# A mixing kernel from four fp32 matmuls over a masked attention, instead of 32 bf16 matmuls over parts that nine transfers spread

## What is computed

```python
h = gelu(embedding @ W0 + b0); h = gelu(h @ W1 + b1)
att = softmax((h @ W2 + b2) / T)                       # (64, 8)
agg_w = einsum('bk,koi->boi', att, weight[..., 0])     # (64, 64, 64)
agg_b = att @ bias_k
mixed = einsum('boi,bih->boh', agg_w, x) + agg_b[:, :, None]
# x + fp8(mixed) @ fp8(weight).T, with one scale for all of `mixed`
# and one for all of the 1024 x 1024 weight (largest absolute value / 448)
```

## Time and profile before

| | |
|---|---|
| runs | 527.64 us median, 527.1 to 528.81 |
| profiled execution | 530.63 us, of which 528.8 us is the span from the first to the last instruction |
| TensorE (PE) | busy 96% of the span, 3480 matmuls |
| VectorE (DVE) | busy 78% |
| ScalarE (ACT) | busy 46% |
| GpSimd (POOL) | busy 11% |
| largest shares of the chain that ended last | PE L1181 40%, PE L1155 19%, PE L1171 15%, DVE L804 5% |

### The profile page before, as it was taken

The page is one execution under the profiler, slowest core; times in us unless marked ns, Lnnn a source line. Parts: engine busy times, 40 slices in busy tenths (PEclk is TensorE's granted clock), DMA queues, the critical chain, the costliest instruction groups (busy, mean ns, idle before and its releaser), DMA issues.

```text
span 528.8 us, 9489 instructions
## 1 busy us (share of the span) xinstructions
PE 510.2 (96%) x3480; PEld 284.7 (54%) x3512; DVE 414.1 (78%) x524; ACT 244.2 (46%) x286; POOL 59.3 (11%) x68
## 2 busy tenths in 40 slices
PE   5799999899999999999999999999999999999997
PEld 4444454355555555555555555555555555555563
DVE  7799999877877777777777777777777777777652
ACT  3469898655344444444444444444444444442310
POOL 5266776011000000000000000000000000000000
PEclk9999999999999999999999999999999999999999
DMA  7999591146666666665656565656656666566532
GB/s 220 382 390 403 206 337 55 58 103 134 189 199 187 183 185 184 182 180 180 180 180 180 180 180 180 180 180 180 180 180 180 183 182 180 181 189 190 193 121 79
DMA packets 85651, 100.61 MB, mean 190 GB/s; under 512 B 34468, under 2 KB 67046, under 8 KB 85638
## 3 DMA queue, kind: packets, MB, share of 16 engines
q1 hardware_dynamic: 84610, 99.41, 59.9%
q0 software_dynamic: 656, 0.82, 0.9%
q10 hardware_dynamic: 372, 0.20, 0.1%
HBM read 58.41 MB, written 32.75 MB: 172 GB/s over the span
## 4 chain that ended last, share of the span: by engine, by line
PE 77%; DVE 12%; DMA 4%; issue 3%; SPq 2%; ACT 1%; POOL 1%; ACTq 0%; DVEq 0%; POOLq 0%
PE pair L1181 40%; PE pair L1155 19%; PE pair L1171 15%; DVE stat L804 5%; DMA Y<-in_L_ffn_weight_dram 2%; DMA work<-work 2%; PE pair L1055 1%; DVE work L729 1%; DVE work L819 1%; DVE work L921 1%; DVE Y L819 1%; DVE work L732 1%; PE pair L1145 1%; SPq L336 1%; POOL fixed L489 1%
## 5 line engine op out<-in xcount | busy, mean ns | idle before, releaser
L1181 PE MATMUL pair<-f1T,work 128*128 128x512 f16 x1024 | 231.0, 379 | 0.0
L1181 PEld LDWEIGHTS pair<-f1T,work 128*128 128x128 f16 x1024 | 98.9, 98 | 113.5 <-DVE work L928 0.2
L608 ACT ACTIVATE work<-Y,consts 128x1024 bf16 (+1 forms) x29 | 33.3, 1148 | 185.7 <-DVE work L902 185.7
L921 DVE TENSOR_TENSOR work<-Y,work 128x512 f16<-128x512 f16 (+1 forms) x64 | 71.2, 1119 | 48.0 <-ACT work L641 46.9
L1155 PE MATMUL pair<-f0T,work 128*128 128x512 bf16 x435 | 98.6, 379 | 1.8 <-DMA work<-work 0.3
L1171 PEld LDWEIGHTS pair<-taps,work 128*128 128x128 f16 x1536 | 88.3, 98 | 8.7 <-issue 0.9
L1171 PE MATMUL pair<-taps,work 128*128 128x128 f16 x1536 | 91.2, 219 | 0.6 <-issue 0.5
L934 DVE TENSOR_TENSOR Y<-pair,Y 128x512 f32 (+1 forms) x64 | 43.9, 686 | 44.4 <-PE pair L1181 44.4
L641 ACT CAST work<-Y 128x512 f16 (+1 forms) x64 | 69.6, 1137 | 19.3 <-DVE Y L911 15.6
L1155 PEld LDWEIGHTS pair<-f0T,work 128*128 128x128 bf16 x464 | 45.3, 98 | 55.1 <-DMA work<-work 0.6
L1055 PE MATMUL pair<-Y,work 128*128 128x512 f32 x128 | 61.2, 613 | 0.4 <-ACT Y L581 0.4
(11 more groups left out here) (157 smaller groups left out, 242.4 us busy)
## 6 DMA issues: line engine op xcount, KB each, us to landing
Y<-in_x_dram SPq DMA_DIRECT2D x64, 512.0 KB, 3.9
out_dram<-Y SPq DMA_DIRECT2D x31, 512.0 KB, 3.8
split_rows<-work SPq DMA_DIRECT2D x30, 520.0 KB, 2.6
work<-split_rows SPq DMA_DIRECT2D x30, 520.0 KB, 3.9
Y<-in_L_ffn_weight_dram SPq DMA_DIRECT2D x8, 512.0 KB, 9.0
Y<-in_L_ffn_W_q_dram SPq DMA_DIRECT2D x5, 512.0 KB, 15.1
work<-in_L_ffn_W_q_dram SPq DMA_DIRECT2D x3, 512.0 KB, 15.2
work<-work SPq DMA_DIRECT2D x8, 65.0 KB, 3.9
```

The lines of the kernel that those rows point to most:

```text
L921: nc.vector.tensor_tensor(split[:, r, s, 1], v[:, r, :], split[:, r, s, 0], ALU.subtract)\
L1181: last = mm(ps[2 + h][:, :], y1s[n][:, e, k, :], f1T[:, k, h * H:(h + 1) * H], start=False, stop=(e == 1 and k == KT - 1), skip_group_chec ...
```

## The change

The expert weights stay as loaded, in 64 partitions, one for a pair of expert `k` and group `c`. The attention is written eight times over (`attR`, 64 columns `(k c)`), turned once, and multiplied by a mask `own_c` (1 where the row's group is `c`) into `attM`, 64 rows by `(c, sample)` = 512 columns. One fp32 matmul for each 128 columns of `wkf`, four in all, then contracts over the 64 rows; a row contributes to its own group's columns alone. The split into bf16 parts, the nine transfers and the fillers behind the softmax fall away.

```diff
-            return pair[m][par * C:(par + 1) * C, :].rearrange("p (j t b) -> p b t j", t=T, b=NB)[:, b]
+            return pair[m][par * C:(par + 1) * C, :].rearrange("p (q c t b) -> p b t q c", q=2, c=KC, t=T)[:, b]
...
-        turns0 = {3 * r + 6: r for r in range(R8)}
+        turns0 = {3 * r + 7: r for r in range(R8)}
... SP
             for r in range(3):
                 load_w0(r)
-            for e in range(2):
-                sp.wait_ge(wk_parts, (1, 3)[e])
-                for i in range(3):
-                    sp.dma_start(wkp9[3 * i + e:KP:9, :], wkp[:, e, :]).then_inc(ld["wkp"], 16)
             load_w0(3)
+            load_mixing(0)
+            sp.wait_ge(mbk_zero, 1)
+            for b in range(NB):
+                sp.dma_start(mbk2[0:KR:KC, b * C:(b + 1) * C], cbk).then_inc(ld["mbk"], 16)
             load_w0(4)
-            for b in range(NB):
-                sp.dma_start(mbk2[:, b * C:(b + 1) * C], cbk).then_inc(ld["mbk"], 16)
             load_w0(5)
-            load_mixing(0)
+            load_mixing(1)
             load_w0(6)
             load_w0(7)
...
-                if n == 3:
+                if n == 5:
                     sp.wait_ge(mix_mm, 2)
+                    sp.wait_ge(mlp_mm, 6)
... POOL (its two loads of convw move ahead of the identity)
+            nc.gpsimd.memset(mbk2, 0.0).then_inc(mbk_zero, 1)
...
-            pool.wait_ge(wk_parts, 4)
-            for i in range(3):
-                pool.dma_start(wkp9[3 * i + 2:KP:9, :], wkp[:, 2, :]).then_inc(ld["wkl"], 16)
... ACT (its load of wkf moves behind the four small ones)
-            for m, par in ((0, 0), (0, 1), (1, 0)):
+            for m in range(2):
                 act.wait_ge(mix_mm, m + 1)
                 for b in range(NB):
-                    ev = nc.scalar.copy(mix_dst(m, par, b), mix_src(m, par, b))
+                    ev = nc.scalar.copy(mix_dst(m, 0, b), mix_src(m, 0, b))
...
-                if t == 2:
+                if t == 5:
                     act.wait_ge(w_step, 2)
-                if t % 3 == 2 and t <= 20:
-                    scale_w0(t // 3 + 1)
+                if t % 3 == 2 and 5 <= t <= 23:
+                    scale_w0(t // 3)
... DVE
+            nc.vector.tensor_reduce(own_c, ident[0:KR, 0:KR].rearrange("p (k c) -> p c k", k=K), AX.X, ALU.add)\
+                .then_inc(own_made, 1)
...
-            nc.vector.tensor_scalar(att, ex, rinv, None, ALU.mult).then_inc(mlp_ev, 1)
+            nc.vector.tensor_scalar(attR.rearrange("p (k c) -> p k c", k=K),
+                                    ex.unsqueeze(2).to_broadcast([B, K, KC]), rinv, None, ALU.mult).then_inc(mlp_ev, 1)
+            dve.wait_ge(mlp_mm, 5)
+            dve.wait_ge(own_made, 1)
+            nc.vector.tensor_tensor(attM, ps[6][0:KR, 256:256 + B].unsqueeze(1).to_broadcast([KR, KC, B]),
+                                    own_c.unsqueeze(2).to_broadcast([KR, KC, B]), ALU.mult).then_inc(mlp_ev, 1)
...
-            for r in range(1, 5):
-                largest_w0(r)
-            place_last()
-            for r in range(5, R8):
+            largest_w0(1)
+            largest_w0(2)
+            for m in range(2):
+                place_odd(m)
+            for r in range(3, R8):
                 largest_w0(r)
... PE
             for q in range(4):
-                for j in range(8):
-                    o2 = 8 * q + j
-                    last = mm(ps[q][:, j * B:(j + 1) * B], wkp9[:, o2 * 2 * C:(o2 + 1) * 2 * C],
-                              attpT, start=True, stop=True)
+                last = mm(ps[q][:, :], wkf[:, q * 2 * C:(q + 1) * 2 * C], attM.rearrange("p c b -> p (c b)"),
+                          start=True, stop=True)
...
-                    if t == 1 and h == 0:
-                        pe.wait_ge(w_red, R8 + 2)
-                        mm(ps[7][:, 128:129], ones, w_all, start=True, stop=True).then_inc(w_pe, 1)
+                    if t == 3 and h == 0:
+                        pe.wait_ge(w_red, R8 + 1)
+                        nc.tensor.transpose(ps[7][0:1, 0:P], w_part, ident[:, :]).then_inc(w_pe, 1)
...
-            keep_clock(10)
-            pe.wait_ge(placed_act, 3)
-            pe.wait_ge(placed_dve, 1)
+            pe.wait_ge(placed_act, 2)
+            pe.wait_ge(placed_dve, 2)
             for t in range(T):
                 mixed_tile(t)
-                if t == 0:
-                    pe.wait_ge(w_red, R8 + 1)
-                    nc.tensor.transpose(ps[7][0:1, 0:P], w_part, ident[:, :]).then_inc(w_pe, 1)
-                if t == 1:
+                if t == 3:
+                    pe.wait_ge(w_red, R8 + 2)
+                    mm(ps[7][:, 128:129], ones, w_all, start=True, stop=True).then_inc(w_pe, 1)
```

More of the change, by code:

```diff
@@ L81, in mix_src @@
         def mix_src(m, par, b):
-            return pair[m][par * C:(par + 1) * C, :].rearrange("p (j t b) -> p b t j", t=T, b=NB)[:, b]
+            return pair[m][par * C:(par + 1) * C, :].rearrange("p (q c t b) -> p b t q c", q=2, c=KC, t=T)[:, b]
         def mix_dst(m, par, b):
-            o = b * C + 32 * m + par
-            return mixw[b * C:(b + 1) * C, :, o:o + 31:2]
+            rows = mixw[b * C:(b + 1) * C, :, b * C:(b + 1) * C]
+            return rows.rearrange("p t (c m q o) -> p m o t q c", c=KC, m=2, q=2)[:, m, par]
         def held(eng, value):
@@ L106, in adaln_ffn_kernel @@
         mixw = work[:, 0:T * P].rearrange("p (t m) -> p t m", t=T)
-        KP = 9 * K
-        wkp9 = Y[0:KP, 20 * L:22 * L].bitcast(bf16)
         KC = C // K
         KF = C * C // KC
[L113 to L118, removed]
+        KR = K * KC
+        wkf = work[0:KR, 5 * L:5 * L + KF]
+        attM = work[0:KR, 6 * L:6 * L + KC * B].rearrange("p (c b) -> p c b", c=KC)
         wide_taps = f0T[:, 0, 0:CG * R8 * 4].bitcast(fp32).rearrange("p (c j) -> p c j", c=CG)
@@ L130, in adaln_ffn_kernel @@
         mw2 = mlp[:, 832:840]
-        att = mlp[0:B, 840:848]
-        attT = mlp[0:K, 848:912]
+        attR = mlp[0:B, 848:848 + KR]
+        own_c = mlp[0:KR, 912:912 + KC]
         rowb = mlp[0:1, 976:984]
@@ L137, in adaln_ffn_kernel @@
         convraw = work[:, 9088:9088 + CG * TAPS].rearrange("p (c k) -> p c k", c=CG)
-        mbk2 = f0T[0:K, R8 - 1, 0:2 * P].bitcast(fp32)
+        mbk2 = f0T[0:KR, R8 - 1, 0:2 * P].bitcast(fp32)
         zs = small[:, 7 * P:8 * P]
@@ L202, in taps_part @@
             return taps16[:, e, :, :, 4 * q:4 * q + 4].rearrange("p h g r a -> p (h g) r a")
-        ld = {n: sem("ld_" + n) for n in ("emb", "mw0", "mw1", "mw2", "ctw", "mbk", "wk", "wkp", "wkl", "fcol", "zs", "b0", "b1",
+        ld = {n: sem("ld_" + n) for n in ("emb", "mw0", "mw1", "mw2", "ctw", "mbk", "wk", "fcol", "zs", "b0", "b1",
                                           "convw", "window")}
@@ L220, in adaln_ffn_kernel @@
         mlp_ev = sem("mlp_ev")
-        wk_parts = sem("wk_parts")
+        own_made = sem("own_made")
+        mbk_zero = sem("mbk_zero")
         taps_made = sem("taps_made")
@@ L348, in _ @@
                 for t in range(2 * n + 1, 2 * n + 3):
-                    load_mixing(t)
-                if n == 3:
+                    if t > 1:
+                        load_mixing(t)
+                if n == 5:
                     sp.wait_ge(mix_mm, 2)
+                    sp.wait_ge(mlp_mm, 6)
                 load_w1(n)
@@ L445, in _ @@
         def _(pool):
+            for b in range(NB):
+                pool.dma_start(convraw[b * C:(b + 1) * C], convw).then_inc(ld["convw"], 16)
             nc.gpsimd.memset(ident[:, :], 0.0).then_inc(ident_zero, 1)
@@ L536, in _ @@
         def _(act):
-            act.dma_start(wkf, cwk.rearrange("k (c o) i a -> (k c) (o i a)", c=KC)).then_inc(ld["wk"], 16)
             row = lambda a: a.rearrange("(a n) -> a n", a=1)
@@ L741, in clear_mixw @@
                 nc.vector.memset(mixw[:, n * R8:(n + 1) * R8, :], 0.0).then_inc(mixw_zero, 1)
[L743 to L752, removed]
+            clear_mixw(0)
+            clear_mixw(1)
+            dve.wait_ge(ident_made, 1)
+            nc.vector.tensor_reduce(own_c, ident[0:KR, 0:KR].rearrange("p (k c) -> p c k", k=K), AX.X, ALU.add)\
+                .then_inc(own_made, 1)
+            clear_mixw(2)
+            clear_mixw(3)
             def largest_w0(r):
@@ L785, in scales, with place_odd @@
                 dve.wait_ge(step, 2)
-            def place_last():
+            def place_odd(m):
                 dve.wait_ge(mixw_zero, 4)
-                dve.wait_ge(mix_mm, 2)
+                dve.wait_ge(mix_mm, m + 1)
                 for b in range(NB):
-                    ev = nc.vector.tensor_copy(mix_dst(1, 1, b), mix_src(1, 1, b))
+                    ev = nc.vector.tensor_copy(mix_dst(m, 1, b), mix_src(m, 1, b))
                 ev.then_inc(placed_dve, 1)
@@ L1024, in _, with turned_tap_rows @@
             keep_clock(16)
-            pe.wait_ge(att_parts, 4)
-            nc.tensor.transpose(ps[1][:, :].bitcast(bf16)[0:KP, 0:B], attp9,
```

(22 more changed lines are left out.)

24 lines of the change are left out of this document (3 added, 21 removed).

## The result

The change takes **532.22 us** (median of 5 runs, 531.91 to 534.23) against 527.64: ratio 1.0094 [1.0069, 1.0119]. It is slower by 4.6 us, outside the range that was given. The profiled execution took 533.73, its span is 531.3.

What follows compares the result with a forecast made beforehand. The prediction took a weight transfer to bound the first stage until 24.1 us, then DVE from the weight's scale on. Gains of 0.8 (earlier scale) and 0.56 (end wait) made 1.4 off 527.64: 526.2 us, range 524.6 to 529.3.

Steps and rivals of the forecast that it cites:

- The nine transfers: First-stage queue: dropping them brings later transfers 5.6 us forward; last weight piece lands at 19.8, tile 3 at 23.9.
- The rival that the nine cost only their bytes: First-stage queue: only 1.5 us saved, tile 3 lands at 28.0, S 30.4, time 530.4; chance 0.08.
- I take 16, because they run without a pause: End of the four mixing matmuls on PE: 16 us, between 14.2 at the full clock and 17.6 at half.
- the forecast's own slow case: Mixing matmuls at the half clock to their end, tiles at full: PE is last and S = 26.9.
- S: Moment DVE makes the weight's scale in the first stage: 27.1 before, forecast 26.3, a gain of 0.8 us.
- The placing copies: Behind the mixing matmuls: two on ACT at 0.63 each, two on DVE at 0.70, ready at 17.7.
- The fourth rival: The change gives nothing: placing copies' four-part strides make the second pair take 2.8, not 1.4; 527.3 in the middle; chance 0.10.
- What comes last: Before S: tile 3 of x, landing at 23.9, is last, after DVE's maxima (23.6) and PE's tiles 0 to 2 (22.9).
- The first rival: PE's half clock holds into the tile mixing until 24.2: S = 29.3, time 529.3, slower by 1.6; chance 0.15.
- The third rival: Queue gains more: tile 3 lands by 22.5, matmuls at full clock, DVE's maxima bind; S = 24.9, time 524.9; chance 0.17.
- The sum against the median: Whole kernel: 1.4 us gain taken from the median 527.64, 3.0 below the profiled execution's 530.63, giving 526.2.
- Behind S and the tail: After S: other edits cost nothing; DVE's 0.56 us wait for PE before the last three maxima goes, lower bound 0.

Runs made afterwards that it cites:

- c0_before: The kernel before, unchanged, run and profiled again: 528.47 us over 12 runs, profiled execution 527.69.
- e3_rows128: The change with its four mixing matmuls over 128 rows instead of 64, the added rows being zeros: 529.73 us, ratio 1.0021 to the kernel before.
- e12: e10 without the fillers ahead of tiles 20 and 21: 527.11 us, ratio 0.9959 to the kernel before.
- e2_endfill: The change with eight filler matmuls of 512 columns where PE idles at the first stage's end: 532.11 us, ratio 1.0075 to the kernel before.
- e1: The change with PE turning the last weight piece before tile 28 again, not behind it: 533.97 us, ratio 1.0099 to the kernel before.
- e4: The change with the placing copies' two inner loops exchanged, writing neighbours 8 bytes apart within a pair: 532.55 us, one execution.
- e6: The change with the turn and spreading of the weight's maxima a tile earlier, behind half of tile 2: 533.31 us, ratio 1.0093 to the kernel before.
- e9: The change with e4's copy loops and e2_endfill's fillers, matmuls still over 64 rows: 532.42 us, ratio 1.0065 to the kernel before.
- e5: The change with the placing copies' tile loop innermost, writing in steps of 512 bytes: 531.28 us, one execution.
- e7: The change with 128-row matmuls, e4's loops, ten fillers before the first tile, the fourth weight maximum before placing, and e2_endfill's fillers: 528.87 us, ratio 1.0002.
- e10: e7 with the maxima's turn and ACT's zeros copy a tile earlier, and fillers ahead of tiles 20 and 21: 526.27 us, ratio 0.9947 to the kernel before.
- e11: e7 with 10 and 20 fillers ahead of tiles 20 and 21: 529.49 us, ratio 1.0014 to the kernel before.

## Why the prediction was wrong

- **The nine transfers: right.** The last piece and tile 3 landed at 19.4 and 23.2. The rival that the nine cost only their bytes, with tile 3 at 28.0, is refuted. In c0_before the same reckoning gives 3.6 instead of 5.6 for the nine, and tile 3 lands at 27.3, so their size varies between executions; 27.3 less 1.5 is still far from 23.2.
- **"I take 16, because they run without a pause": the step that failed.** The matmuls ended at 17.65, the worse of the two ends. What stood ahead of the rise in the kernel before were turns, fillers and most of a tile over 128 rows; four matmuls over 64 rows are no substitute, and e3_rows128 shows that in one edit. The same step let the tiles run at the full level. They were at the lower one until 23.0, and the 14 passes took 7.72 us, not 6.1. Even the forecast's own slow case, the matmuls at the lower level to their end and the tiles at the full one, gave S = 26.9. That is 2.2 too early: 1.6 for these passes, 0.8 for their start, at 20.02 and not 19.3, less 0.2 for the turn and the spreading.
- **The placing copies: a term mis-sized.** Costed at 0.63 and 0.70 as before, they take 1.08 and 1.09. That is most of the 0.8 of the tiles' start. The new step of the writes stood in the diff. The fourth rival had this at up to twice the price, with little weight.
- **What comes last.** Tile 3's transfer should have been last. It was PE, by its own work: 17.65, 19.84, 20.02 + 7.72, S 29.06. The first rival had this mechanism, and its working gave 29.3; it was given 0.15. That its S came so near is in part luck: it had the copies too short (placing ready at 19.2, measured 19.84) and the rise too late (24.2, measured 23.0). Its time, 529.3, was too low by the next point.
- **The third rival's sum.** The maxima of DVE at 21.8 would give S = 23.3 with the 1.5 for turn and spreading. The 24.9 that stands there is tile 3 landing at 22.5, not DVE.
- **The sum against the median.** "The median of the runs is 3.0 lower, and against it the forecast is" treats the 3.0 as lying outside the terms. c0_before shows 2.1 of it in S. Against 25.0 even the forecast's own S of 26.3 is a loss of 1.3, and by its own terms the forecast would have been 527.64 + 1.3 - 0.56 = 528.4. With S at 29.06 and the measured tail it would be 527.6 + 4.0 - 0.9 = 530.7. The remaining 1.5 is not settled. The profile puts 1.3 on the low clock behind the stage's end, four of the five executions have such a fall, and in e12 the executions with one take 1.5 longer than those without. But e2_endfill, with one in seven, had nearly the same median.
- **Behind S and the tail: right.** No wait of DVE in the rounds, the tail's 0.56 gone, 0.9 in all, against both traces of the kernel before. Not seen: an engine that gets ahead at the end stands longer (1.82 instead of 0.96).

Left open: what sets off a fall of the clock. It followed waits of PE of 1.8 to 2.7 us in the change, e1, e3, e4, e6 and e9. But e5 has the same wait of 1.81 us at the stage's end as the change and no fall, and in e7, e10, e11 and e12, with e2's fillers and no wait of PE above 0.5 us there, the clock fell at 95.9 to 99.5 too. Nor was it tried whether the kernel before gains by fillers at its own stage end.

## What to carry to other kernels

Before fewer, wider matmuls replace many small ones while the engine is still at its lower clock, ask what raised the clock until now: here a contraction over half the partitions did not, and zeros in the other half were worth 2.5 to 3.8 us. When a sum starts at one profiled execution that is slower than the median, find in a second trace which term holds the excess. And when a step moves, move with it the small work of other engines that is placed by the same tile number: one copy left a tile behind cost 2.1 us.

## What the runs showed of the hardware that was not expected

- fp32 matmuls of 512 columns over 64 rows ran from 10.48 to 17.65, 0.90 a pass, without a rise of the clock (the same in all eight traces with 64 rows); over 128 rows the clock was full from 12.7, and from 11.0 to 14.2 in the six traces with 128 rows. Only 64 and 128 rows were tried.
- ACT and DVE copies of 64x512 fp32 from PSUM to SBUF: 0.63 and 0.70 where the written elements are 8 bytes apart, in a row or in pairs; 1.08 and 1.09 where they are 32 apart, 1.03 to 1.10 where they are 512 apart.
- The clock fell again in the middle of the work, at 101.5 in the change, at 73.0 in e1, at 95.9 in e12, and each time cost PE 1.2 to 1.7 us; in e12, six executions with a fall took 1.5 us longer than six without. Fillers at one place (e2) went with fewer falls, but the median stayed.
